# Third stage of a fused graph network: feed-forward products in fp32r parts, residual by transposes, another order, and the head mask added by VectorE

## The reference

```python
def _gat_heads(x, adj, W, a):
    Wh = einsum('bnf,hfo->bhno', x, W)
    f1 = einsum('bhno,ho->bhn', Wh, a[:, :O]);  f2 = einsum('bhno,ho->bhn', Wh, a[:, O:])
    e = f1[:, :, :, None] + f2[:, :, None, :]
    e = where(e > 0, e, 0.01 * e)
    e = where(adj[None, None] > 0, e, -1e9)
    return einsum('bhnm,bhmo->bhno', softmax(e, axis=-1), Wh)

h = elu(_gat_heads(enc_inputs, adj, W_heads, a_heads))        # 4 heads
h = transpose(h, (0, 2, 1, 3)).reshape(B, N, -1)
out = elu(_gat_heads(h, adj, W_out[None], a_out[None])[:, 0]) # 1 head
ffn = maximum(out @ w1 + b1, 0.0) @ w2 + b2
y = ffn + out
return (y - mean(y)) / sqrt(var(y) + 1e-5) * ln_gamma + ln_beta
# outside: x = x + that
```

## Time and profile before

| what | value |
|---|---|
| median of 3 runs | 1637.37 us (1637.23 to 1638.43) |
| profiled execution: its own time / its span | 1637.47 us / 1635.7 us |
| PE busy in the span | 1449.0 us, 89% |
| DVE busy | 1202.6 us, 74% |
| ACT busy | 1024.2 us, 63% |
| POOL busy | 454.5 us, 28% |
| mean granted TensorE clock | 0.967 |
| third stage | from 613 us to about 1488 us |

### The profile page before, as it was taken

One profiled execution on the slowest core, in us unless ns is written; L12 is line 12 of the kernel. 1 busy time (PEld: TensorE's weight loads), 2 busy tenths in 40 slices (PEclk: granted clock), 3 DMA queues, 4 the chain that ended last, 5 costly groups with the idle time before them and its releaser, 6 DMA issues.

```text
span 1635.7 us, 36230 instructions
## 1 busy us (share of the span) xinstructions
PE 1449.0 (89%) x11581; PEld 1276.4 (78%) x11645; DVE 1202.6 (74%) x2747; ACT 1024.2 (63%) x3241; POOL 454.5 (28%) x747
## 2 busy tenths in 40 slices
PE   5689999999879987999999999999999999965776
PEld 4578888888769985888888888888888888854554
DVE  4877777767657766777878787787878778743887
ACT  3568878878735546666656566665656666522776
POOL 1122222222036652122223132222313222122332
PEclk9889999999969997999999999999999999996999
DMA  7400000000000000000000000000000000000112
GB/s 238 136 2 0 0 0 0 0 0 0 1 1 0 0 0 1 1 1 1 1 0 0 0 0 0 0 0 0 0 0 0 0 0 1 1 1 7 65 64 71
DMA packets 23873, 24.23 MB, mean 15 GB/s; under 512 B 1936, under 2 KB 23184, under 8 KB 23696
## 3 DMA queue, kind: packets, MB, share of 16 engines
q1 hardware_dynamic: 23824, 23.60, 4.6%
HBM read 15.21 MB, written 8.39 MB: 14 GB/s over the span
## 4 chain that ended last, share of the span: by engine, by line
PE 43%; DVE 26%; ACT 17%; issue 12%; DVEq 1%; POOL 1%; DMA 0%; ACTq 0%; SPq 0%; POOLq 0%
ACT probs L877 9%; PE bank L1433 4%; DVE em L690 4%; PE bank L1337 4%; PE bank L1372 4%; PE bank L1141 3%; DVE probs L702 2%; PE bank L1234 2%; PE bank L1225 2%; DVE st L248 2%; PE bank L1393 2%; PE bank L1266 2%; PE bank L1279 2%; PE bank L1278 2%; PE bank L1280 2%
## 5 line engine op out<-in xcount | busy, mean ns | idle before, releaser
L877 ACT ACTIVATE probs<-bank,negtop 128x128 f32<-128x128 f32 x512 | 185.8, 415 | 48.0 <-DVE negtop L630 48.0
L275 POOL TENSOR_TENSOR var_eps<-mv,eps_tile 128x2 f32<-128x2 f32 x128 | 48.5, 379 | 590.7 <-DVE mv L263 590.7
L291 ACT ACTIVATE h<-x_all,shift,rstd 128x256 f32 (+1 forms) x256 | 140.0, 597 | 33.1 <-POOL shift L281 33.1
L1350 PE MATMUL bank<-wout_hi,headsT_hi 128*128 128x258 f32 x512 | 150.5, 294 | 0.0
L1350 PE MATMUL bank<-wout_lo,headsT_hi 128*128 128x258 f32 x512 | 144.4, 282 | 0.0
L1350 PE MATMUL bank<-wout_hi,headsT_lo 128*128 128x258 f32 x512 | 144.2, 282 | 0.0
L966 ACT ACTIVATE em<-bank 128x512 f32<-128x512 f32 x128 | 75.7, 591 | 98.9 <-PE bank L1337 98.5
L487 POOL TENSOR_TENSOR var_y<-mv_y,eps_tile 128x2 f32<-128x2 f32 x32 | 8.8, 276 | 463.1 <-DVE mv_y L756 463.1
L1337 PE MATMUL bank<-probsT,whs 128*128 128x128 f32 x1024 | 132.8, 278 | 0.0
L877 ACT ACTIVATION_READ_ACCUMULATOR probs<-bank,negtop 128x1 f32 x512 | 130.0, 254 | 0.0
L1337 PEld LDWEIGHTS bank<-probsT,whs 128*128 128x128 f32 x1024 | 125.9, 194 | 2.7
(11 more groups left out here) (215 smaller groups left out, 4638.3 us busy)
## 6 DMA issues: line engine op xcount, KB each, us to landing
x_all<-in_x SPq DMA_DIRECT2D x32, 256.0 KB, 2.8
out_x<-x_all SPq DMA_DIRECT2D x32, 256.0 KB, 2.1
wh<-in_L_gnn_W_heads SPq DMA_DIRECT2D x2, 512.0 KB, 7.9
a_heads<-in_L_gnn_a_heads SPq DMA_DIRECT2D x1, 1024.0 KB, 11.1
wout<-in_L_gnn_W_out SPq DMA_DIRECT2D x1, 1024.0 KB, 10.8
raw<-in_L_gnn_W SPq DMA_DIRECT2D x1, 512.0 KB, 5.3
ffn<-in_L_gnn_w SPq DMA_DIRECT2D x2, 256.0 KB, 7.2
consts<-in_shape_consts SPq DMA_DIRECT2D x1, 322.0 KB, 2.8
```

The costliest lines, as they stand in the source:

```text
L291: last = nc.scalar.activation(h[:, p, c, :], x_all[:, bass.ds(g * G + c, 1), :].rearrange("p a d -> p (a d)"), ACT.Relu, bias=shift[:, p, ...
L877: last = nc.scalar.activation(probs[:, r, i, :], bank[4 + r][:, i * N:(i + 1) * N], ACT.Exp, bias=negtop0[:, r, i:i + 1], scale=float(DH) ...
L1350: last = nc.tensor.matmul(bank[5 + c][:, 0:D + 2], src[:, i, o, c, :], w[:, k, :], start=(k == 0 and src is headsT_hi and w is wout_hi), s ...
```

## The change

In the third stage:

- Head scores: TensorE no longer adds the mask. f1 and f2 are split by VectorE (`f_high`, `f_part`) and both parts lie in different rows of `left` and `right`, now fp32r, so that one fp32r product gives the score. The mask is added in `soft(c)` by a `tensor_tensor` of VectorE.
- Feed-forward: both weights, `outT` and `uT` are split in parts on ScalarE and VectorE; each product is made of three fp32r passes. The residual is four transposes ahead of the second product.
- `y`: the work of L784, L494 and L497 is now four `scalar_tensor_tensor` of VectorE; POOL has only the bias and the small statistics.
- Order: in a step, the last head (`l`) goes earlier on PE, ACT and DVE, the first feed-forward product is made ahead of `out_product(3)`, and its split, relu and second split lie in the same step on DVE, ahead of the normalisation of `y`.
- Some buffers share memory that had their own; weights of the feed-forward part are split once, in an early step.

```diff
-                    dve.wait_ge(soft2, g * 4 + c * 2 + 1)
+                    dve.wait_ge(soft2, g * 6 + c * 3 + 1)
+                    nc.vector.tensor_tensor(probs[:, c], probs[:, c], hide2[:, :, :], ALU.add).then_inc(soft2, 1)
+                    dve.wait_ge(soft2, g * 6 + c * 3 + 2)
...
-                    nc.vector.tensor_scalar(left[:, :], bank[0][0:64, 0:N], left_mul[0:64], left_add[0:64], ALU.mult, ALU.add)
+                    nc.vector.tensor_copy(f_high[:, :], bank[0][0:64, 0:N]).then_inc(lr_step, 1)
+                    nc.vector.scalar_tensor_tensor(f_part[:, :], f_high[:, :].bitcast(FP32), low_rows[0:64], bank[0][0:64, 0:N],
+                                                   ALU.mult, ALU.add).then_inc(lr_step, 1)
+                    nc.vector.tensor_scalar(left[:, :], f_part[:, :], left_mul[0:64], left_add[0:64], ALU.mult, ALU.add)
...
+                    nc.vector.tensor_copy(outT_hi[:, :, :, :], outT[:, :, :, :]).then_inc(outT_ready, 1)
+                    nc.vector.tensor_tensor(outT_lo[:, :, :, :], outT[:, :, :, :], outT_hi[:, :, :, :].bitcast(FP32),
+                                            ALU.subtract).then_inc(outT_ready, 1)
...
+                    nc.vector.tensor_copy(uT_hi[:, :, :, :], uT[:, :, :, :]).then_inc(u_ready, 1)
+                    nc.vector.tensor_tensor(uT_lo[:, :, :, :], uT[:, :, :, :], uT_hi[:, :, :, :].bitcast(FP32),
+                                            ALU.subtract).then_inc(u_ready, 1)
+                if e:
+                    for c in range(G):
+                        last = nc.vector.scalar_tensor_tensor(y[:, c, :], y[:, c, :], mv_y[:, c, 0:1], gamma_row[:, 0, :],
+                                                              ALU.subtract, ALU.mult)
+                    for c in range(G):
+                        last = nc.vector.scalar_tensor_tensor(xs, y[:, c, :], rstd_y[:, c:c + 1], xs, ALU.mult, ALU.add)
...
+                def residual():
+                    pe.wait_ge(u_relu, ge + 1)
+                            nc.tensor.matmul(bank[7][:, c * D + k * N:c * D + (k + 1) * N], outT[:, k, c, :], ident, is_transpose=True,
+                                             start=(c == 0 and k == 0), stop=False)
+                def second_ffn():
+                    pe.wait_ge(u_ready, ge * 2 + 2)
+                            for src, w in ((uT_hi, ffn2_hi), (uT_hi, ffn2_lo), (uT_lo, ffn2_hi)):
+                                last = nc.tensor.matmul(bank[7][:, c * D:(c + 1) * D], src[:, k, c, :], w[:, k, :], start=False,
+                def scores():
+                        nc.tensor.matmul(bank[1 + c][:, :], left[rows, :], right[rows].rearrange("p h n -> p (h n)"),
+                                         start=True, stop=True).then_inc(s2_full, 1)
...
-                        nc.tensor.matmul(bank[1 + c][:, :], ident_bf[:, :], hide2[:, :, :], start=True, stop=False)
```

More of the change, by code:

```diff
@@ L155, in build_program @@
         p3T = sb("p3T", [N, G, N])
[L156 to L159, removed]
+        outT_hi, outT_lo, uT_hi, uT_lo = [sb(name, [N, KC, G, N], F32R) for name in ("outT_hi", "outT_lo", "uT_hi", "uT_lo")]
         st_y = sb("st_y", [N, G, 6])
@@ L1050, in step2 @@
                         nc.scalar.copy(hi, w).then_inc(w_hi, 1)
+                if n and isinstance(gn, int) and gn == 1:
+                    for hi, w in ((ffn1_hi, ffn1), (ffn2_hi, ffn2)):
+                        nc.scalar.copy(flat(hi), flat(w)).then_inc(w_hi, 1)
                 if m:
@@ new lines, in probs_last, with attend_last @@
+                def probs_last():
+                    pe.wait_ge(p3_ready, gl + 1)
+                    for c in range(G):
+                        last = nc.tensor.transpose(bank[7][:, c * N:(c + 1) * N], t3[:, 0, c, :], ident)
+                    last.then_inc(pT3_full, 1)
+                def attend_last():
+                    pe.wait_ge(pT3_ready, gl + 1)
+                    for o in range(KC):
+                        for c in range(G):
+                            last = nc.tensor.matmul(bank[7][:, (o * G + c) * N:(o * G + c + 1) * N], wh2[:, pl, c, o * N:(o + 1) * N],
+                                                    p3T[:, c, :], start=True, stop=True)
+                    last.then_inc(at3_full, 1)
@@ new lines, in first_ffn @@
+                def first_ffn():
+                    if not positive(gl):
+                        pe.wait_ge(w_lo, 5)
+                    pe.wait_ge(outT_ready, gl * 2 + 2)
+                    for o in range(KC):
+                        for k in range(KC):
+                            for w, src in ((ffn1_hi, outT_hi), (ffn1_lo, outT_hi), (ffn1_hi, outT_lo)):
+                                last = nc.tensor.matmul(bank[7][:, o * G * N:(o + 1) * G * N], w[:, k, o * N:(o + 1) * N],
+                                                        src[:, k].rearrange("p c n -> p (c n)"),
+                                                        start=(k == 0 and w is ffn1_hi and src is outT_hi), stop=(k == KC - 1 and src is outT_lo))
+                    last.then_inc(u_full, 1)
@@ L1368, in step2 @@
                 if e:
-                    pe.wait_ge(u_ready, ge + 1)
-                    for c in range(G):
-                        for k in range(KC):
-                            nc.tensor.matmul(bank[7][:, c * D:(c + 1) * D], uT[:, k, c, :], ffn2[:, k, :], start=(k == 0), stop=False)
-                        for k in range(KC):
-                            last = nc.tensor.matmul(bank[7][:, c * D + k * N:c * D + (k + 1) * N], outT[:, k, c, :], ident,
-                                                    start=False, stop=(k == KC - 1))
-                    last.then_inc(y_full, 1)
+                    residual()
+                    second_ffn()
                 if f:
```

250 lines of the change are left out of this document (134 added, 116 removed).

## The result

The changed kernel takes 1581.35 us in the median of 4 runs (1574.39 to 1582.87), the kernel before 1637.49 beside it: a ratio of 0.9648 (95% interval 0.9619 to 0.9677). The forecast was 1585 us, range 1567 to 1622. The terms behind it were less good than the total: the full steps gained less than forecast, the ends of the stage more.

The account below looks back on a forecast made before the run. Before, a ring through PE and DVE set the step; after, DVE's list would. 28 full steps from 26.01 to 24.0 us save 56, the edges add 4: 1637.5 - 52 = 1585 us, range 1567 to 1622.

Parts of the forecast that it names:

- Who bounds: In a full step the bound was to change sides: DVE would need 23.7 us, PE 22.5.
- the ring: Before: PE from first feed-forward product to scores, about 10 us, then DVE from first `soft` to next `outT`, about 15.
- the two places named: PE's waits for DVE in a full step, ahead of `features` and the second product: some 1.2 us in all.
- PE's work: PE's own work in a full step would fall from 24.6 to about 22.5 us.
- POOL's stall: DVE's L710 and L690 stood still for POOL's L494 and L497: 2.2 us a full step, to disappear.
- Scores' operands: On DVE in a full step: `f_high` and `f_part` +0.86 us, `left` and `right_rows` -0.24, sum +0.62.
- rival 1: POOL's L304 starts before the second mask, DVE stands about 1.1 us a step: 25.1 us, 1616 in all; chance 0.13.
- The step: A full step takes 24.0 us, DVE's list of 23.7 plus 0.3, instead of 26.01: 56 us less over 28.
- tight hand-offs: In a full step, two hand-offs to DVE met by less than 0.15 us; with three waits before `y`, 0.3 added.
- The edges: Eight steps at the stage's ends: +4 us in all, between -6 (all hidden) and +12 (all exposed).
- rival 2: Waits appear on DVE, a hand-off missed by 1 to 1.5 us each step: 25.3 us, 1622 in all; chance 0.15.
- rival 3: The split comes too late for PE, DVE waits at three places: 26.4 us a step, 1652 in all; chance 0.08.

Follow-up runs that it names:

- a3: Changed kernel with DVE's subtraction for `uT_lo` made twice, 0.72 us more on DVE a step: 1602.30 us, ratio 0.9790.
- b2: Changed kernel with the eight transposes of the head probabilities made twice, 0.87 us more on PE a step: 1579.27 us, ratio 0.9661.
- a4: Kernel before, with only the normalisation of `y` moved to DVE and POOL's two instructions gone: 1604.83 us, ratio 0.9806.
- e2: Changed kernel with constants in place of the two per-partition operands of `y`, so its normalisation is left out: 1574.18 us, ratio 0.9611.
- c2: Changed kernel with the mask on PE again and both feed-forward products in fp32 without splits: 1568.20 us, ratio 0.9579.
- b3: Kernel before, with only the mask moved to DVE: 1684.81 us, ratio 1.0293.
- a2: Changed kernel with both feed-forward products in fp32 again, without the splits of `outT` and `uT`: 1555.57 us, ratio 0.9506.
- e1: Changed kernel with only the first feed-forward product in fp32 again, without the split of `outT`: 1554.90 us, ratio 0.9499.
- e4: Changed kernel with DVE's copy of `wh` put between the two pairs of `y`: 1572.32 us, ratio 0.9597.

## Why the prediction was right, step by step

- **Who bounds**: right. The bound went from the ring to DVE's own list (a3, b2), and PE is the one that waits, with 1.25 and 0.22 us at the two places named.
- **PE's work**: 22.99 us busy, against 22.5; the prices of the passes, 0.12 us, and of the scores (0.43 us against 0.46) held. Of the 0.5 us more, 0.1 is the first pass of the second product (0.23 us instead of 0.12); the rest was not traced to a term. It counts for nothing here, as PE waits.
- **DVE, the terms**: masks 2 x 0.69 us, copies 0.42: right. POOL's stall of 2.2 us: right and shown by a4. Scores' operands: some 0.05 us a step under the estimate, as two errors nearly cancel: `f_high` and `f_part` take 0.32 and 0.37 us from start to start (0.43 each in the forecast), `left` and `right_rows` 0.63 together (0.51).
- **DVE, the term that was mis-sized**: `y`, taken at 1.42 us from L760's 0.40, is 1.92 in the mean of its two forms. Of the 0.50 us, 0.24 are the pause (0.32 and 0.15 us by turns) and the rest the per-partition operands, which L760 does not have (e2).
- **A term that was left out**: POOL's L309 meets not a mask but L699, for 0.26 us a step. It is the mechanism of rival 1 on an instruction that I had not looked at; I only asked whether the masks were safe.
- **The step**: the list 23.7, plus 0.50 and 0.26, less 0.05, is 24.4, as measured. The 0.3 us that I added for tight hand-offs was for something that did not occur; it stood in the place of less than half of these two. Full steps: 28 x 1.61 = 45 us in place of 56.
- **The edges**: the step that failed. I took +4 us, between -6 and +12; it is -11, outside even that range. First four steps: -2.6 (76.9 us in place of 79.5 from the start of the stage to `hT2_lo` of the first full step). End of the stage: -8.7 (from `hT2_lo` of the last full step to the first statistics of the fourth stage 78.4 us in place of 88.6: 10.3 less, of which 1.6 belong to that full step). Two more differences between the profiled executions are no effect of the change that can be told: the third stage starts 2.3 us earlier (first `hT2_lo` at 615.23; it lies anywhere from 613.4 to 617.5 us in the kernels here, whose first two stages are alike), and the fourth takes 2.2 us longer (149.9; 147.7 to 150.1 in the kernels here).
- **Why the edges**: I had priced the splits as exposed there. c2, which has neither the splits nor the masks on DVE, has nearly the same edges: -3.3 at the start and -8.1 at the end. So the named parts, splits against shorter products and all, add up to about nothing at the edges, and the gain is from the parts that c2 keeps. One of them is `y` on DVE, without L494 and L497: a4 alone has -0.3 and -5.4. The other 3.0 and 2.7 us of c2 were not divided between order, transposed residual and scores; that the new order shortens the distances from engine to engine for the last head and the first product is a guess.
- **Two errors of 11 and 15 us with opposite signs** leave 4 us between forecast and result. That the total is so close is luck: the range held it with room, but the terms do not give it.
- **Rivals 1, 2 and 3**: not in this kernel. That DVE waits for no other engine in a full step excludes 2 and 3. On rival 1 the prediction's argument was wrong, to the safe side: it called the distance from the aggregation to POOL's beta addition fixed, at 1.35 us, and it is 2.06 (1019.93 to 1021.99), as L493 and L495 take 0.55 and 1.14 us where L487 and L489 took 0.28 and 0.70. The mask starts 1.21 us ahead of L309, where under half a microsecond was forecast, and ends 0.52 us ahead of it; b3 shows what lies on the other side. The Trainium skill, "VectorE: DVE Perf Modes", section "The perf-mode tier table", has the copy at two elements in a cycle; the trace agrees with 0.42 us for 512 columns where `tensor_tensor` takes 0.69. The Trainium skill, "GPSIMD Engine Reference", section "Specifications", has GpSimd contend with instructions of VectorE with two SBUF inputs; the trace agrees, as such an instruction of 0.69 us took 1.67 (b3) to 1.79 us.

## What to carry to other kernels

When work is moved off the busiest engine, add up both lists after the move: once the receiving engine is the fuller, every further transfer costs its full price, and two edits that each gain alone can lose together (here 12.6 and 11.1 us gained, and 13 us lost). Price the first and last steps of a pipeline by their own chains of hand-offs, not by the list of the full step. And for each GpSimd instruction over two tensors ask, after every change of order, which VectorE instruction it now starts beside, not only whether the one you fear is safe.

## What the runs showed of the hardware that was not expected

- A `scalar_tensor_tensor` of 128x256 takes 0.478 us with a per-partition operand and 0.419 with a constant in its place (e2).
- Between two dependent pairs of it on VectorE a pause appears, in the changed kernel of 0.32 or 0.15 us by turns, in a2, c2, a4 and e1 of 0.30 to 0.32 us throughout; an independent instruction between them fills it (e4, 9 us for the kernel). What makes it 0.32 in one step and 0.15 in the next was not settled.
- An instruction of VectorE that starts within one of GpSimd's over two tensors took 1.67 us in place of 0.69 (b3) where it started 0.29 us behind it, and 0.94 in place of 0.68 (changed kernel) where it started 0.90 us behind it.
- A lower granted clock of TensorE need not lengthen a step: in b3 it was 0.94 in some full steps and 1.00 in others, TensorE was busy for 25.8 and 24.5 us of them, and both took 27.8 us: the longer work filled TensorE's wait of 1.33 us for `outT` (L799), which is in its timeline of a step at 1.00 and not in that of one at 0.94.
